# The input bias of a fused GRU and block-attention kernel, sent by DMA instead of spread by matmuls

## The chip, the cores and the metric

The kernel runs on one core of a Trainium2 chip. The metric is the device time of one execution in microseconds (us), the median of several runs; less is better. One further execution was recorded by the hardware profiler, and every row shown here comes from such a record. The engines are TensorE (PE, its weight loads PEld), VectorE (DVE), ScalarE (ACT), GpSimd (POOL) and SyncE (SP), which here only starts transfers. GpSimd starts a few transfers too, on a queue of its own.

## What is computed

Two layers, each added to its own input; all tensors are float32. The first is a GRU over 64 steps, the second an attention over blocks of 8 steps with a projection and a layer norm.

```python
# x: [32, 64, 512]; cond: [32, 512]; W_ih, W_hh: [512, 1536]
def cell(h, x):
    gi = x @ W_ih + b_ih
    gh = h @ W_hh + b_hh
    i_r, i_z, i_n = split(gi, 3); h_r, h_z, h_n = split(gh, 3)
    r, z = sigmoid(i_r + h_r), sigmoid(i_z + h_z)
    n = tanh(i_n + r * h_n)
    return (1 - z) * n + z * h
x = x + scan(cell, cond, x)           # h of each step
block = x.reshape(32, 8, 8, 512).sum(2)
keys = rmsnorm(block @ Wk.T) * rms_weight
attn = softmax(keys @ cond[1])
proj = (attn-weighted sum of block) @ Wo.T
out = x + layernorm(x + proj) * gamma + beta
```

## The kernel before

The recurrence sets the length. A step `t` works on a 128 x 128 state: partition `j*32 + b` holds 128 of the 512 units of batch row `b`. For each step TensorE runs 16 matmuls of `h_t` (the transposed state) with `w_hh` into a bank of PSUM (`step`, L608), which is `first_ps[t]` for the first four steps and `gates_ps` for the rest. Then the gates are made by ScalarE and VectorE. While they are, TensorE computes the input's share `gi` of the step five ahead (`gi_chunk`, L571): 12 matmuls of 384 columns, from `x` and `W_ih` each split into a high and a low part, into one of two banks `gi_ps`. VectorE adds the bias tile `b_in` and moves the result to `gi_tok` (`keep_gi`, L723). SyncE moves that by DMA, SBUF to SBUF, from time-major rows to the state's layout in `gi` (`move_gi`, L240). At the end of a step ScalarE writes the next step's `gi` and bias into `gates_ps` (`seed_n`, L427, and `seed_rz`, L436), and TensorE accumulates on top.

The first four steps take their `gi` another way: the bias is laid into the four banks `first_ps[0..3]`, and the products of `x` and `W_ih` are accumulated straight onto it in full float32 (L635, four rounds `k` of 16 matmuls, each round waiting for its quarter of `W_ih`).

The two biases come in as 8 rows (`bias_rows`, 4 for `b_ih`, 4 for `b_hh`), loaded by two small DMAs into zeroed memory. A first matmul with K = 8 (`own_rows` as weights, L624) puts them in the state's layout into `first_ps[0]`; ScalarE copies that to `bias_rec`, and from there ScalarE and VectorE seed the other three banks. Behind the rounds of `W_ih` four more matmuls with K = 8 (`pick` as weights, L638) spread the rows over all 128 partitions, one chunk of 384 columns each, and ScalarE copies the four results to `b_in` (L423). TensorE waits for all four copies before the first `gi_chunk` (for step 4), and VectorE before the `keep_gi` of it.

Transfers before the first step all go through SyncE's queue in this order: the biases, `x` of the first four steps, `cond`, the four quarters of `W_ih` (768 KB each), `x` of the next four (`load_ahead(1)`), the four quarters of `W_hh`. Some wait for an earlier one to land. Then come, step by step, the moves of `gi`, the loads of `x_t` ahead, and `x1`, the same input in the other layout (`load_residual`). GpSimd waits for the last quarter of `W_hh` (L363) and then starts six transfers that copy small rows to many partitions: `gamma`, `beta`, `wq_rec`, `keys_wq`, `keys_sq` and `wq` (L368 to L372).

Places that matter to the order in time:

- Step 4 is the first that is seeded from `gi`. At `s = 3` ScalarE waits, ahead of `seed_rz`, until four moves have landed, those of steps 4, 5, 6 and 7 (L434).
- `gi_tok` has two halves. The `keep_gi` of step 6 waits until the move of step 4 has landed, that of step 7 waits for the move of step 5, and so on.
- SyncE starts its transfers in program order: move of step 4, load of `x_t`, moves of 5 and 6, load of `x1`, move of 7.

## Time and profile before

| | us |
|---|---|
| median of 3 runs | 407.91 (406.82 to 408.11) |
| profiled execution, device time | 407.7 |
| its span, first to last instruction | 405.9 |
| TensorE busy | 365.0 (90%) |
| VectorE busy | 286.1 (70%) |
| ScalarE busy | 138.0 (34%) |
| GpSimd busy | 62.1 (15%) |

In this execution the gates of step 0 begin at 29.69 us, and those of steps 1 to 4 follow at 5.00 us intervals. What comes before 29.69 us is the opening; what comes after about 346 us is attention and layer norm. All times in the sections below are us from the start of the span.
### The profile page before, as it was taken

To read this page: it belongs to the slowest core of one execution; us is meant where nothing else is said; L and a number is where in the kernel's file an instruction comes from. 1 tells how busy PE (TensorE), PEld (TensorE's weight loads), DVE (VectorE), ACT (ScalarE), POOL (GpSimd) and SP (SyncE) were. 2 spreads that over 40 slices of the span, in tenths; PEclk is the share of its full clock that TensorE was granted. 3 is DMA by queue.
4 is the path that set the end of the run, shared out by engine and by line. 5 is a ranking of instruction groups with operands and counts; after the bars stand their busy time and mean duration, and the time that the engine had idled before them with its cause. 6 is when DMAs were issued, how large, how long until landed. Compare 5 with 4: busy or idle time off the path is not lost.

```text
span 405.9 us, 9319 instructions
## 1 busy us (share of the span) xinstructions
PE 365.0 (90%) x3102; PEld 212.4 (52%) x3102; DVE 286.1 (70%) x1191; ACT 138.0 (34%) x498; POOL 62.1 (15%) x74
## 2 busy tenths in 40 slices
PE   6999999999999999999999999999999999755400
PEld 2455565656565656565656565656565643422100
DVE  1605577776777767777676767676767666999997
ACT  5411223232323232323232323232323553545532
POOL 5040010101010101000010001010101010263563
PEclk9969999999999999999999999999999999996955
DMA  6936525322222222222222221313132210000233
GB/s 265 409 46 105 152 83 159 78 65 67 66 65 65 65 65 65 65 65 65 66 63 70 59 79 51 82 48 82 53 76 60 51 41 27 2 1 1 104 156 155
DMA packets 17412, 33.89 MB, mean 84 GB/s; under 512 B 2088, under 2 KB 9904, under 8 KB 17392
## 3 DMA queue, kind: packets, MB, share of 16 engines
q1 hardware_dynamic: 16912, 32.85, 27.2%
q0 software_dynamic: 480, 0.79, 1.8%
q8 instruction: 10, 0.16, 0.2%
q14 instruction: 10, 0.08, 0.1%
HBM read 17.64 MB, written 4.19 MB: 54 GB/s over the span
## 4 chain that ended last, share of the span: by engine, by line
PE 82%; DVE 14%; POOL 1%; issue 1%; ACT 0%; POOLq 0%; DVEq 0%
PE gates_ps L608 40%; PE gi_ps L571 34%; DVE cx_all L990 5%; DVE cx_all L1011 2%; PE first_ps L635 1%; DVE cx_all L1039 1%; PE fourth_ps L635 1%; PE third_ps L635 1%; PE keys_ps L635 1%; DVE w_hh L982 1%; PE fourth_ps L608 1%; PE third_ps L608 1%; PE keys_ps L608 1%; PE first_ps L608 1%; DVE w_hh L976 1%
## 5 line engine op out<-in xcount | busy, mean ns | idle before, releaser
L608 PE MATMUL gates_ps<-w_hh,h_t 128*32 128x384 f32 x1920 | 167.3, 489 | 0.7 <-DVE h_t L745 0.6
L608 PEld LDWEIGHTS gates_ps<-w_hh,h_t 128*32 128x32 f32 x1920 | 56.7, 109 | 82.9 <-issue 50.8
L571 PE MATMUL gi_ps<-w_ih_hi,xt_hi 128*128 128x384 f32 x240 | 87.7, 365 | 0.6 <-issue 0.6
L467 ACT ACTIVATE rz<-gates_ps 128x256 f32<-128x256 f32 x60 | 23.1, 385 | 173.4 <-PE gates_ps L608 173.4
L571 PE MATMUL gi_ps<-w_ih_hi,xt_lo 128*128 128x384 f32 x240 | 81.2, 338 | 0.0
L571 PE MATMUL gi_ps<-w_ih_lo,xt_hi 128*128 128x384 f32 x240 | 81.2, 338 | 0.0
L823 DVE TENSOR_TENSOR rz<-gates_ps,rz 128x128 f32<-128x128 f32 x60 | 17.5, 292 | 80.2 <-ACT rz L467 80.2
L571 PEld LDWEIGHTS gi_ps<-w_ih_hi,xt_hi 128*128 128x128 f32 x240 | 45.5, 189 | 39.0 <-issue 39.0
L353 POOL TENSOR_TENSOR xb_all<-x,beta 128x512 f32 (+1 forms) x16 | 21.2, 1327 | 187.9 <-DVE x L753 187.9
L571 PEld LDWEIGHTS gi_ps<-w_ih_lo,xt_hi 128*128 128x128 f32 x240 | 45.7, 190 | 0.0
L571 PEld LDWEIGHTS gi_ps<-w_ih_hi,xt_lo 128*128 128x128 f32 x240 | 45.6, 190 | 0.0
L723 DVE TENSOR_TENSOR gi_tok<-gi_ps,b_in 128x384 f32<-128x384 f32 x60 | 33.0, 550 | 12.6 <-PE gi_ps L571 12.6
L745 DVE STREAM_TRANSPOSE h_t<-hist 128x32 f32<-128x32 f32 x189 | 36.4, 216 | 2.4 <-issue 0.2
L739 DVE TENSOR_TENSOR hist<-zh,n 128x32 f32<-128x32 f32 (+1 forms) x192 | 34.2, 201 | 2.2
L732 DVE SCALAR_TENSOR_TENSOR n<-rz,n 128x32 f32<-128x32 f32 (+1 forms) x192 | 31.0, 189 | 0.0
L476 ACT ACTIVATE n<-n 128x32 f32<-128x32 f32 (+1 forms) x128 | 29.0, 256 | 3.3 <-DVE n L828 3.3
L427 ACT ACTIVATE gates_ps<-bhh_n 128x128 f32<-128x128 f32 x60 | 16.9, 282 | 21.5 <-DVE rz L823 21.5
L436 ACT ACTIVATE gates_ps<-gi 128x256 f32<-128x256 f32 x60 | 22.5, 375 | 1.8
L828 DVE TENSOR_TENSOR n<-rz,gi 128x32 f32<-128x32 f32 x120 | 21.6, 222 | 0.0
L395 POOL TENSOR_TENSOR cx_all<-cx_all,xb_all 128x1024 f32<-128x1024 f32 x7 | 17.5, 2501 | 16.4 <-DVE cx_all L990 15.4
L359 POOL COPY br_all<-br_cur 128x128 f32 x7 | 2.0, 291 | 99.8 <-DVE br_turned L777 99.8
L829 DVE TENSOR_TENSOR zh<-rz,hist 128x96 f32<-128x96 f32 x64 | 16.1, 251 | 0.0
(210 smaller groups left out, 338.4 us busy)
## 6 DMA issues: line engine op xcount, KB each, us to landing
gi<-gi_tok SPq DMA_DIRECT2D x60, 192.0 KB, 3.3
x<-in_x_rec_dram SPq DMA_DIRECT2D x16, 256.0 KB, 2.8
x_t<-in_x_t_dram SPq DMA_DIRECT2D x15, 256.0 KB, 3.3
out_dram<-cx_all SPq DMA_DIRECT2D x7, 512.0 KB, 2.6
xb_all<-in_w_ih_dram SPq DMA_DIRECT2D x4, 768.0 KB, 6.0
w_hh<-in_w_hh_dram SPq DMA_DIRECT2D x4, 768.0 KB, 7.0
wo_t<-in_wo_t_dram SPq DMA_DIRECT2D x1, 1024.0 KB, 5.6
wk_t<-in_wk_t_dram SPq DMA_DIRECT2D x1, 1024.0 KB, 5.6
```

What stands on the lines that cost most here:

```text
L353: pool.tensor_tensor(xb_all[:, bass.ds(quad * Q, Q), :], x1[:], over_steps(beta), ALU.add).then_inc(xb_ready, 1)
L436: act.activation(gates_ps[:, P:3 * P], gi[:, (s // Q) % 2, first + P:first + G3], ACT.Copy).then_inc(seeded, 1)
L467: act.activation(rz[:], gates_bank(t)[:, P:3 * P], ACT.Sigmoid).then_inc(rz_ready, 1)
L476: act.activation(n[:, c], n[:, c], ACT.Tanh).then_inc(n_ready, 1)
L571: mm = pe.matmul(gi_ps[tok][:, 0:G3], a[:, k, :], w[:, k, gi_cols(j)], start=(k == 0 and a is xt_hi and w is w_ih_hi), stop=(k == NJ - 1 a ...
L608: mm = pe.matmul(gates_bank(t)[j * B:(j + 1) * B, P:], h_t[:, k * B:(k + 1) * B], chunk(w_hh, k, j), start=False, stop=(k == NJ - 1), skip ...
L723: dve.tensor_tensor(gi_tok[:, tok, :], gi_ps[tok][:, 0:G3], b_in[:, gi_cols(j)], ALU.add).then_inc(gi_tok_ready, 1)
L732: dve.scalar_tensor_tensor(out=n[:, c], in0=z[:, c], scalar=1.0, in1=n[:, c], op0=ALU.subtract, op1=ALU.mult).then_inc(terms_ready, 1)
L739: dve.tensor_tensor(hist[:, s, c], zh[:, c], n[:, c], ALU.subtract).then_inc(h_ready, 1)
L745: dve.transpose(h_t[:, c], hist[:, s, c]).then_inc(ht_ready, 1)
L828: dve.tensor_tensor(n[:, c], r[:, c], i_n[:, c], ALU.add).then_inc(n_pre_ready[number], 1)
L990: ins = dve.scalar_tensor_tensor(out=cx_all[:, c * C + t, :], in0=u_of(c, t), scalar=rstd[:, c * C + t:c * C + t + 1], in1=gamma[:], op0=A ...
```

## The change

- **`b_in`**: the four `pick` matmuls, their four ScalarE copies and the `pick` tile are gone. SyncE, once the second quarter of `W_hh` has landed, starts two transfers behind the queued quarters: `b_ih` (6 KB in memory) copied to 128 partitions, and the r and z parts of `b_hh` (four pieces of 1 KB) copied to 128 partitions. GpSimd adds the second to the first, 128 x 1024 elements, and signals `b_in_ready`. This addition stands ahead of GpSimd's six transfers.
- **`keep_gi(Q, Q)`** on VectorE (for step 4) moves from before step 0 to after step 0's last transpose, together with the wait for `b_in_ready`. TensorE no longer waits for `b_in` before the first `gi_chunk`.
- **The remaining bias matmul** gets `own_rows` and `bias_rows` of 128 partitions, zero beyond the first 8. VectorE clears `bias_rows` (128 x 512), after `zeros` and before it makes the zero operand `xt_hi`; the first bias load waits for that.
- **Zero matmuls**: two of 512 columns before the bias matmul and six behind it, into `gates_ps`, which nothing reads before step 4. `split_x(1)` on ScalarE waits for the six, since it overwrites their operand.
- The copy to `bhh_n` on ScalarE moves behind the splits.

```diff
-        bias_rows = xb_all[0:2 * NJ, 48:52, :].rearrange("p t u -> p (t u)")
+        bias_rows = xb_all[:, 48:52, :].rearrange("p t u -> p (t u)")
...
-        pick = cx_all[0:2 * NJ, 2 * NJ:3 * NJ, :]
-        own_rows = cx_all[0:2 * NJ, 3 * NJ + 1, :]
+        own_rows = cx_all[:, 3 * NJ + 1, :]
+        b_hh_rz = cx_all[:, 5 * NJ:7 * NJ, :].rearrange("p (j c) u -> p j (c u)", j=NJ)
...
             load_w_hh(3)
+            sp.wait_ge(w_hh_in[1], 16)
+            sp.dma_start(b_in[:], b_ih_d.rearrange("j n -> (j n)")[None, :].broadcast_to([P, 3 * D])
+                         ).then_inc(b_in_loaded, 16)
+            sp.dma_start(b_hh_rz, b_hh_d[None, :, 0:2 * P].broadcast_to([P, NJ, 2 * P])).then_inc(b_in_loaded, 16)
             move_gi(0, -1)
...
+            pool.wait_ge(made, 6 + 1 + 2 * NJ)
+            pool.wait_ge(b_in_loaded, 32)
+            rz_cols = b_in[:].rearrange("p (j n) -> p j n", j=NJ)[:, :, P:]
+            pool.tensor_tensor(rz_cols, rz_cols, b_hh_rz, ALU.add).then_inc(b_in_ready, 1)
             pool.wait_ge(w_hh_in[NJ - 1], 16)
...
-            act.activation(bhh_n[:], bias_rec[:, 3 * P:], ACT.Copy)
...
+            act.wait_ge(pe_warmed, Q + 1)
             split_x(1)
-            for j in range(NJ):
-
-                act.wait_ge(bias_spread, j + 1)
-                act.activation(b_in[:, gi_cols(j)], bias_ps[j][:, 0:G3], ACT.Copy).then_inc(b_in_ready, 1)
+            act.activation(bhh_n[:], bias_rec[:, 3 * P:], ACT.Copy)
...
-            pe.wait_ge(pick_made, 6)
+            def keep_warm(times):
+
+                for _ in range(times):
+                    mm = pe.matmul(gates_ps[:], xt_hi[:, 0, :], xt_hi[:], start=True, stop=True)
+                return mm
+
+            keep_warm(2)
+            pe.wait_ge(pick_made, 3)
             pe.wait_ge(bias_in, 32)
             pe.matmul(first_ps[0][:], own_rows, bias_rows, start=True, stop=True).then_inc(bias_laid, 1)
+            keep_warm(6).then_inc(pe_warmed, 1)
...
-            for j in range(NJ):
-                pe.matmul(bias_ps[j][:], pick[:, j, :], bias_rows, start=True, stop=True).then_inc(bias_spread, 1)
 
             pe.wait_ge(made, 6 + 1 + 2 * NJ)
-            pe.wait_ge(b_in_ready, NJ)
             gi_chunk(Q, Q, 1)
...
+                if peeled and s == 0:
+                    dve.wait_ge(b_in_ready, 1)
+                    keep_gi(Q, Q)
                 if not (last and t + 5 >= T):
                     keep_gi(t + 5, s + 5)
...
             dve.memset(zeros, 0.0).then_inc(zeros_made, 1)
+            dve.memset(bias_rows, 0.0).then_inc(bias_made, 1)
...
             split_x(1)
-            dve.wait_ge(b_in_ready, NJ)
-            keep_gi(Q, Q)
```

On TensorE, at the start of the program, the four zero matmuls, the bias matmul and the first round of `W_ih` stand like this before:

```order
L621 MATMUL first_ps<-xt_hi 128x512
L624 MATMUL first_ps<-xb_all,cx_all 128x512
L635 MATMUL first_ps<-xb_all,cx_all 32x384 x4
L635 MATMUL keys_ps<-xb_all,cx_all 32x384 x4
L635 MATMUL third_ps<-xb_all,cx_all 32x384 x4
```

and after:

```order
L622 MATMUL first_ps<-xt_hi 128x512
L626 MATMUL gates_ps<-xt_hi 128x512 x2
L632 MATMUL first_ps<-xb_all,cx_all 128x512
L626 MATMUL gates_ps<-xt_hi 128x512 x6
L644 MATMUL first_ps<-xb_all,cx_all 32x384 x4
L644 MATMUL keys_ps<-xb_all,cx_all 32x384 x4
```

Two zero matmuls came in ahead of the bias matmul and six behind it; nothing else moved there.

On TensorE again, between the last round of `W_ih` and the first `gi_chunk`, before (`cx_all` holds `pick`, `xb_all` the bias rows):

```order
L635 MATMUL fourth_ps<-xb_all,cx_all 32x384 x4
L638 MATMUL gates_ps<-xb_all,cx_all 128x512
L638 MATMUL gi_ps<-xb_all,cx_all 128x512 x2
L638 MATMUL small_ps<-xb_all,cx_all 128x512
L571 MATMUL gi_ps<-w_ih_hi,xt_hi 128x384
L571 MATMUL gi_ps<-w_ih_lo,xt_hi 128x384
```

and after:

```order
L644 MATMUL third_ps<-xb_all,cx_all 32x384 x4
L644 MATMUL fourth_ps<-xb_all,cx_all 32x384 x4
L572 MATMUL gi_ps<-w_ih_hi,xt_hi 128x384
L572 MATMUL gi_ps<-w_ih_lo,xt_hi 128x384
L572 MATMUL gi_ps<-w_ih_hi,xt_lo 128x384
```

The four spreading matmuls are gone, and the chunk of step 4 follows the last round directly.

On GpSimd, behind the making of the constants, before:

```order
L348 MEMSET own_n 32x1
L368 DMA gamma<-in_gamma_dram 128x1x128
L368 DMA beta<-in_beta_dram 128x1x128
L368 DMA wq_rec<-in_rms_weight_dram 128x1x128
L368 DMA keys_wq<-in_cond_dram 128x1x128
L369 DMA keys_sq<-in_cond_dram 128x4x128
L372 DMA wq<-in_rms_weight_dram 128x512
```

and after:

```order
L348 MEMSET own_n 32x1
L366 TENSOR_TENSOR b_in<-b_in,cx_all 128x4x256
L372 DMA gamma<-in_gamma_dram 128x1x128
L372 DMA beta<-in_beta_dram 128x1x128
L372 DMA wq_rec<-in_rms_weight_dram 128x1x128
L372 DMA keys_wq<-in_cond_dram 128x1x128
L373 DMA keys_sq<-in_cond_dram 128x4x128
L376 DMA wq<-in_rms_weight_dram 128x512
```

The addition came in ahead of the six transfers, and they now stand behind its wait for the two new loads.

## Rows read from the trace of the kernel before

**Rows 1.** The page's part 4, the chain that ended last, by engine.

```profile
PE 82%; DVE 14%; POOL 1%; issue 1%; ACT 0%; POOLq 0%; DVEq 0%
```

**Rows 2.** Timeline, VectorE's first two, then TensorE: start, duration, operation, idle before.

```profile
0.84 0.17 DVE L877 MEMSET cx_all<- 128x128 f32 x1 [0.84 <-PEq L1048]
1.04 0.50 DVE L879 CAST xt_hi<-cx_all 128x512 fp32r<-128x512 f32 x1
...
4.37 2.07 PE L624 MATMUL first_ps<-xb_all,cx_all 8*128 8x512 f32 x2 [0.71 <-POOL cx_all L327]
...
7.22 1.51 PE L635 MATMUL first_ps<-xb_all,cx_all 128*32 128x384 f32 x8 [0.78 <-ACT cx_all L409]
...
12.33 0.89 PE L635 MATMUL first_ps<-xb_all,cx_all 128*32 128x384 f32 x8
...
14.97 0.83 PE L635 MATMUL first_ps<-xb_all,cx_all 128*32 128x384 f32 x8
...
20.25 1.12 PE L638 MATMUL gates_ps<-xb_all,cx_all 8*128 8x512 f32 x2
...
25.68 0.66 PE L571 MATMUL gi_ps<-w_ih_hi,xt_hi 128*128 128x384 f32 x1 [0.63 <-issue]
...
29.69 2.79 PE L608 MATMUL first_ps<-w_hh,h_t 128*32 128x384 f32 x32
```

**Rows 3.** Timeline around the start of step 4: TensorE, VectorE, SyncE, ScalarE.

```profile
49.69 2.79 PE L608 MATMUL gates_ps<-w_hh,h_t 128*32 128x384 f32 x32
...
45.10 0.52 DVE L723 TENSOR_TENSOR gi_tok<-gi_ps,b_in 128x384 f32<-128x384 f32 x1
...
45.65 0.55 SPq L240 DMA_DIRECT2D gi<-gi_tok  x1
...
49.04 0.39 ACT L436 ACTIVATE gates_ps<-gi 128x256 f32<-128x256 f32 x1
```

**Rows 4.** Busy time by stretch: PE, PEld, DVE, ACT, POOL, granted clock, DMA share, GB/s.

```profile
17.00:20.00 3.00, 3.00 (x44) 1.31 (x36) 0.23 (x1) 0.00 (x0) 0.00 (x0) 1.00 1.02 417
20.00:21.00 1.00, 1.00 (x6) 0.48 (x3) 0.00 (x0) 0.00 (x0) 0.00 (x0) 1.00 0.24 98
...
23.00:24.00 1.00, 1.00 (x2) 0.33 (x1) 0.00 (x0) 0.49 (x1) 1.00 (x2) 0.50 0.00 0
...
29.00:30.00 1.00, 1.00 (x7) 0.51 (x10) 0.13 (x1) 0.00 (x0) 0.00 (x0) 0.74 1.41 61
```

**Rows 5.** GpSimd's first transfer in the timeline, and its groups by form (busy, mean ns).

```profile
22.75 0.89 POOL L368 DMA_DIRECT2D gamma<-in_gamma_dram  x1 [15.15 <-DMA w_hh<-in_w_hh_dram]
...
L395 POOL TENSOR_TENSOR cx_all<-cx_all,xb_all 128x1024 f32<-128x1024 f32 x7 | 17.5, 2501 | 16.4 <-DVE cx_all L990 15.4 <-DVE cx_all L1006 0.9
```

**Rows 6.** Queues by stretch (packets, MB, share of 16 engines): 28 to 34, then 34 to 35.3.

```profile
DMA packets 63, 0.25 MB, mean 41 GB/s; under 512 B 3, under 2 KB 3, under 8 KB 63
q0 software_dynamic: 63, 0.25, 89.2%
...
q0 software_dynamic: 95, 0.26, 51.3%
q1 hardware_dynamic: 110, 0.17, 39.5%
```

**Rows 7.** One `gi` move each: its issue in the timeline, its time to landing.

```profile
30.45 0.69 SPq L240 DMA_DIRECT2D gi<-gi_tok  x1
DMA to landing us min/median/max: 7.0/7.0/7.0
...
DMA to landing us min/median/max: 3.3/3.3/3.3
```

**Rows 8.** Transfers issued from 35 to 38: KB each, time to landing.

```profile
gi<-gi_tok SPq DMA_DIRECT2D x1, 192.0 KB, 4.0
```

**Rows 9.** TensorE late in the kernel, idle before a matmul, and the clock there.

```profile
369.66 0.58 PE L695 MATMUL small_ps<-w_hh,same_b 128*128 128x16 f32 x2 [6.71 <-DVE w_hh L957]
...
367.00:368.00 1.00, 0.00 (x0) 0.00 (x0) 1.00 (x1) 0.00 (x0) 0.57 (x1) 0.72 0.00 0
```

More of the change, by code:

```diff
@@ L140, in gru_block_attention @@
         small_ps, third_ps, fourth_ps = pb("small_ps"), pb("third_ps"), pb("fourth_ps")
-        bias_ps = [gates_ps, gi_ps[0], gi_ps[1], small_ps]
         first_ps = [pb("first_ps"), keys_ps, third_ps, fourth_ps]
@@ L151, in gru_block_attention @@
         gi_moved = [sem("gi_moved0"), sem("gi_moved1")]
-        warmed, bias_spread, bias_laid, bias_kept = sem("warmed"), sem("bias_spread"), sem("bias_laid"), sem("bias_kept")
+        warmed, bias_laid, bias_kept = sem("warmed"), sem("bias_laid"), sem("bias_kept")
+        b_in_loaded = sem("b_in_loaded")
         first_seeded, pe_warmed, zeros_made = sem("first_seeded"), sem("pe_warmed"), sem("zeros_made")
@@ L317, in _ @@
         def _(pool):
-            pool.memset(bias_rows, 0.0).then_inc(bias_made, 1)
-            pool.memset(pick, 0.0).then_inc(pick_made, 1)
             pool.memset(own_rows, 0.0).then_inc(pick_made, 1)
@@ L322, in _ @@
             for half_ in range(2):
-                pool.wait_ge(pick_made, 2 + 2 * half_)
+                pool.wait_ge(pick_made, 1 + half_)
                 pool.affine_select(out=own, in_=own, compare_op=ALU.not_equal, fill=1.0, base=-NJ * half_,
                                    pattern=[[-1, NJ], [0, B]], channel_multiplier=1).then_inc(pick_made, 1)
-                pool.affine_select(out=pick, in_=pick, compare_op=ALU.not_equal, fill=1.0, base=-NJ * half_,
-                                   pattern=[[-1, NJ], [0, P]], channel_multiplier=1).then_inc(pick_made, 1)
             pool.memset(ident[:], 0.0).then_inc(made, 1)
```

## The prediction

> **What bounds the kernel now.** I read the chain of waits first [rows 1]: TensorE holds 82% of it, and in the recurrence it works through 5.00 us steps without a gap (the gates of step 0 begin at 29.69, those of step 4 at 49.69 [rows 2, 3]). The change touches nothing inside a step, so it can only move the moment from which the steps run at that pace. I therefore read TensorE's timeline from the start [rows 2]. The opening has three costs. The first round of `W_ih` takes 5.1 us (7.22 to 12.33) where the next takes 2.64 (to 14.97): the engine had worked without a break for 5.1 us before its matmuls came at double pace. The four K=8 matmuls and the wait for their copies take from 20.1 (the end of the rounds, 12.33 + 3 x 2.6) to 25.68. And behind them the first `gi_chunk` runs at half pace, 4.0 us (25.68 to 29.69) instead of about 2.1: the granted clock was 0.50 in 23 to 24, after 3 us of 8-row matmuls, and 0.74 in the stretch in which it rose again [rows 4]. Step 0's gates then end at 29.69 + 2.79 = 32.48. I call that G0; step 4's gates begin 17.2 us behind it [rows 3]. A price for the end of the kernel is read at step 4, because from there on nothing of the opening is left.
>
> **TensorE's own part.** Without the spreading the chunk follows the rounds, and at full clock: 20.1 + 2.1 = 22.2, gates to 25.0. G0 comes 7.5 us sooner, if nothing else is late.
>
> The zero matmuls move the clock's rise. VectorE now clears 128 x 512 elements ahead of the zero operand. No row shows that; the nearest are its 128x128 clear (0.17 us) and its copy of that shape (0.50) [rows 2], so 0.17 to four times that. I take 0.5, like the copy: the zero operand is ready at 2.1, and the first bias load, issued at 1.3 now, leaves 0.3 later and all loads behind it too. Six zero matmuls of 512 columns at 1.2 GHz, 0.43 each, end at 4.7, the bias matmul (2.07 [rows 2]) at 6.7, 0.3 later than now. TensorE then goes on with six zeros instead of pausing 0.78. It has worked from 2.1 nearly without a break, so by the 5.1 us before 12.33 and the 4.0 us before 29.69 it rises at 6 to 7; most of the six then take half as long and end near 7.9, inside the wait for the seeds (8.5). Rounds: 8.5 to 18.3, the chunk to 20.4. If the clock rises as late as now, the zeros cost 1.6 us and the rounds end at 20.9, G0 25.8. Either way the fourth quarter of `W_hh` has to be there: it lands now at 22.5, 0.25 before GpSimd's first transfer [rows 5], which will be 22.8. So G0 = 22.8 + 0.65 (the last quarter of the gates) + 0.1 = 23.6 in the good case, **8.9 us sooner**. The padded rows cost nothing: matmul time goes by columns here, 8 or 128 rows.
>
> **The bias by DMA, and who waits.** The two loads carry 128 x 6 KB + 128 x 4 KB = 1.31 MB. They stand behind the `W_hh` quarters on a queue that is full until 20.2 (417 GB/s) with a few late packets afterwards [rows 4]; the late ones are why the last quarter lands only at 22.5. At 417 GB/s they need 3.15 us more, landing at 22.8 + 3.15 = 25.95. GpSimd starts 0.25 later and adds 1024 elements in 2.5 us, as in its 128x1024 group [rows 5]: `b_in_ready` at **28.75**. VectorE waits for it between step 0 and step 1, with both `keep_gi` and step 1's elementwise work queued behind. Both must be through when step 1's gates are, at G0 + 5.5; two times 0.55 us for `keep_gi` leaves a deadline of G0 + 4.4. With G0 = 23.6 this is missed by 0.75, so the steps run as if G0 were 24.35, 8.1 us sooner than now. In the late-clock case (G0 25.8) the deadline is met.
>
> **What is late next.** GpSimd's six transfers stand behind the addition. They begin at 28.75 instead of 22.75, 6.0 us later, while the steps run 8.1 earlier; they slide 14 us into the steps. Their queue q0 [rows 6] is slow in one part: from 28 to 34 it moved 0.25 MB at 41 GB/s with the engines 89% taken (this is `keys_sq`, four pieces of 512 B copied to all partitions), and its last 0.26 MB went in 34 to 35.3. Meanwhile SyncE's queue moved nothing: the `gi` move issued at 30.45 needed 7.0 us to land, an undisturbed one 3.3 [rows 7]. Shifted by 6.0, q0 is done at 41.3 and blocks from about 32.6. The move of step 4 (issued 29.3), `x_t` and the move of step 5 (30.5) should just go ahead of it. The move of 6, `x1` and the move of 7 do not; these are 640 KB. ScalarE seeds step 4 only when the moves up to step 7 have landed. In the trace that is barely met today: `keep_gi` at 45.10, issue 45.65, seed 49.04, gates of step 4 at 49.69 [rows 3]. Now these 640 KB start behind q0. At the 331 GB/s of 34 to 35.3 they would be in by 43.3; the same mix (move, `x_t`, move) took until 35.65 + 4.0 = 39.65 in the trace [rows 8], 4.35 us behind q0's end, which gives 45.65. I take 45.2, near that row, since the last move is queued already. With 0.1 + 0.39 + 0.05 for the seed, **step 4's gates begin at 45.75** instead of 49.69.
>
> The sum, against the profiled execution: 407.7 - (49.69 - 45.75) = 403.8. The runs' median is 0.2 above that execution: **404.0 us**. More than half of the 8 us won on TensorE goes into a new wait in front of step 4, about 4.2 us long (from 24.35 + 17.2 = 41.55). The late-clock case gives the same time, since that wait ends by GpSimd's transfers and not by G0.
>
> **Rivals.**
> 1. SyncE's queue is served beside q0. Against it stands the 7.0 us landing; for it, that one transfer is little evidence. The Trainium skill says so ("DMA: Bandwidth & Descriptors", Queues, rings and completion order): each engine takes turns between its queue rows, packet by packet. This trace doesn't agree, by that 7.0 us. Worked from rows: an engine that alternates passes the moves among the last slow packets and is through with all three transfers some 2.5 us sooner, 401.5; with no slow part at all the 8.1 us remain whole, 399.8. Chance 0.2.
> 2. TensorE's clock falls in the new gap. Late in the kernel TensorE was idle for 6.71 us and the clock fell 4.7 us into it (0.72 in 367 to 368) [rows 9]. The gap here is 4.2, a little under. If it falls, the next 4 to 5 us run at half pace, 2 to 2.5 us: 406.2. Chance 0.12.
> 3. The move of step 5 is caught behind q0 too. Then the `keep_gi` of step 7 waits for it until 41 to 42, where step 3's work on VectorE should begin at 39.8, and everything behind is 1 to 2 us later: 405.5. Chance 0.1.
> 4. Slower than before: the loads of the bias are as slow as `keys_sq`. All four copy a small row to many partitions, and `b_hh`'s part has its form, four pieces for each of 128 partitions. At 41 GB/s its 0.52 MB take 12.8 us instead of 1.3, `b_in_ready` comes 11.5 us later, and with it the six transfers: 415.5. The break-even is 3.9 us of extra loading, 7.1 us for both or 185 GB/s. Against it: `wq` copies a 2 KB row the same way and ran in the fast stretch from 34 to 35.3 [rows 6], and `b_ih` comes in pieces of 6 KB. Chance 0.13, spread from 406.5 upward.
>
> **How the numbers follow.** The forecast has 0.45, the rivals 0.2, 0.12, 0.1 and 0.13. The time is the likeliest case's, 404.0. Its own bounds are 43.3 to 45.65 for the last landing (402.1 to 404.5) and 0.5 us for the clear and the loads. Low end 399.6, from rival 1 whole; high end 408.5, which leaves out most of rival 4. A measurement tells 0.3% (1.2 us) from no change: faster means below 406.7. That is the forecast, rivals 1 and 3 and over half of rival 2: 0.81. Within 0.3%: the rest of 2 and the near part of 4, 0.07. Slower: 0.12.
>
> **What would show it.** In the changed kernel's timeline: rounds of `W_ih` all 2.6 us long, no clock fall before step 0, gates of step 0 ending at 23.5 to 26; the addition on GpSimd starting near 26.2 and lasting 2.5; VectorE waiting for it before the first `keep_gi`; q0 at some 40 GB/s from 34 to 40; a move of `gi` with a landing of 7 us or more; and TensorE waiting some 4 us for ScalarE's seed in front of step 4. Wrong would be: loads landing after 29 (rival 4), no wait in front of step 4 (rival 1), or gates of step 4 drawn out beyond their 2.79 us (rival 2).

## The result, and the profile after

The changed kernel takes 408.8 us (median of 20 runs, 407.16 to 410.61), the kernel before 407.2 us in the same rounds (20 runs, 405.28 to 408.39). The ratio is 1.0046, with a 95% interval of 1.0032 to 1.0060: slower by half a percent, where 404.0 and faster was forecast. The profiled execution took 408.77 us with a span of 407.0, 1.1 us longer than the one of before. The page's part 4 for it, the chain that ended last, beside [rows 1]:

```profile
PE 72%; DVE 15%; DMA 9%; SPq 1%; issue 1%; POOL 1%; ACT 0%; DVEq 0%; ACTq 0%; POOLq 0%
```

TensorE's share fell by ten points and the transfers have 9%, where before they had none. The timeline of TensorE in the changed kernel, which answers to [rows 2] and to the gates in [rows 3] (start, duration, operation, idle time before and what ended it):

```profile
7.60 0.88 PE L644 MATMUL first_ps<-xb_all,cx_all 128*32 128x384 f32 x8
...
10.23 0.87 PE L644 MATMUL first_ps<-xb_all,cx_all 128*32 128x384 f32 x8
...
18.12 0.44 PE L572 MATMUL gi_ps<-w_ih_hi,xt_hi 128*128 128x384 f32 x1
...
20.41 2.14 PE L609 MATMUL first_ps<-w_hh,h_t 128*32 128x384 f32 x24
23.23 0.85 PE L609 MATMUL first_ps<-w_hh,h_t 128*32 128x384 f32 x8 [0.68 <-DMA w_hh<-in_w_hh_dram]
...
36.98 2.79 PE L609 MATMUL fourth_ps<-w_hh,h_t 128*32 128x384 f32 x32
48.30 5.35 PE L609 MATMUL gates_ps<-w_hh,h_t 128*32 128x384 f32 x32 [5.86 <-ACT gates_ps L437]
...
56.01 2.79 PE L609 MATMUL gates_ps<-w_hh,h_t 128*32 128x384 f32 x32
...
347.18 2.79 PE L609 MATMUL gates_ps<-w_hh,h_t 128*32 128x384 f32 x32 [0.21 <-DVE h_t L751]
```

Up to 23.23 everything is as it was meant: the first round of `W_ih` takes 2.63 us instead of 5.1, the chunk follows the rounds, and step 0 begins at 20.41 instead of 29.69. Step 4 begins at 48.30, after 5.86 us of idling, only 1.4 us ahead of before; its gates take 5.35 us instead of 2.79, and by step 5 the kernel is behind. In the kernel before the last step's gates began here:

```profile
345.91 2.79 PE L608 MATMUL gates_ps<-w_hh,h_t 128*32 128x384 f32 x32 [0.21 <-DVE h_t L745]
```

So each execution splits into three numbers: the start of step 4, the 59 steps from there to the last, and the rest. Before: 49.69 + 296.22 + 59.99. After: 48.30 + 298.88 + 59.82. The change won 1.39 us, lost 2.66 us inside the steps behind it, and the small remainder lies in the end.

The other engines of the changed kernel, from its timeline; compare [rows 3] and [rows 5]:

```profile
26.68 2.37 POOL L366 TENSOR_TENSOR b_in<-b_in,cx_all 128x1024 f32<-128x1024 f32 x1 [20.97 <-DMA cx_all<-in_b_hh_dram]
29.00 0.89 POOL L372 DMA_DIRECT2D gamma<-in_gamma_dram  x1
29.08 1.02 DVE L729 TENSOR_TENSOR gi_tok<-gi_ps,b_in 128x384 f32<-128x384 f32 x2 [2.29 <-POOL b_in L366]
...
39.45 0.55 SPq L240 DMA_DIRECT2D gi<-gi_tok  x1
...
47.85 0.39 ACT L437 ACTIVATE gates_ps<-gi 128x256 f32<-128x256 f32 x1 [6.61 <-DMA gi<-gi_tok]
```

The seed of step 4 waited 6.61 us for a move of `gi` to land. That move was issued at 39.45, and the trace has this for it (who waited for it, and the time from issue to landing; undisturbed it is 3.3 [rows 7]):

```profile
  ACT gates_ps L437: 6.6, 1
...
DMA to landing us min/median/max: 8.3/8.3/8.3
```

Meanwhile, from 38 to 42, GpSimd's queue had the 16 transfer engines to itself, 92% busy at 33 GB/s; SyncE's queue moved nothing although the move of index 6, `x1` and, from 39.45, the last move were waiting:

```profile
DMA packets 32, 0.13 MB, mean 33 GB/s; under 512 B 0, under 2 KB 0, under 8 KB 32
q0 software_dynamic: 32, 0.13, 92.4%
```

The times to landing of the two large copies on that queue, changed kernel (source and issuer, count, KB, us to landing):

```profile
keys_sq<-in_cond_dram POOLq DMA_DIRECT2D x1, 256.0 KB, 11.1
wq<-in_rms_weight_dram POOLq DMA_DIRECT2D x1, 256.0 KB, 12.2
```

and before:

```profile
keys_sq<-in_cond_dram POOLq DMA_DIRECT2D x1, 256.0 KB, 9.2
wq<-in_rms_weight_dram POOLq DMA_DIRECT2D x1, 256.0 KB, 9.9
```

And the clock. The changed kernel by stretch, columns as in [rows 4]:

```profile
42.00:46.00 4.00, 0.43 (x3) 0.11 (x1) 0.58 (x5) 0.00 (x0) 0.00 (x0) 1.00 1.03 246
46.00:47.00 1.00, 0.00 (x0) 0.00 (x0) 0.45 (x2) 0.00 (x0) 0.00 (x0) 0.93 1.03 237
47.00:48.00 1.00, 0.00 (x0) 0.00 (x0) 0.97 (x2) 0.15 (x1) 0.16 (x1) 0.50 1.03 367
50.00:53.00 3.00, 3.00 (x24) 0.79 (x16) 0.00 (x0) 0.00 (x0) 0.00 (x0) 0.50 0.36 74
54.00:55.00 1.00, 1.00 (x8) 1.00 (x7) 0.87 (x6) 0.64 (x4) 0.00 (x0) 1.00 0.00 0
```

TensorE had been idle since 42.4; its clock fell from 2.4 to 1.2 GHz at 46.9 (a mean of 0.93 in 46 to 47), 4.4 us into the gap, and it was back by 54. Step 4's gates ran at half speed.

One point of the description of the kernel before has to be put right, since the experiments lean on it. `gi_chunk` of index 4 to 7, and the move of each, do not hold the input's share of step 4, 5, 6, 7. Each holds one quarter of the columns for all four steps. That is why the seed of step 4 needs all four moves; the wait can't be relaxed step by step. The waits and their times are as described. In what follows the four are called the moves 4 to 7.

### The profile page after: what moved, and what is told of

It is laid out like the page before. It is cut to its first block, busy times and chain, and to the rows that moved or that the text cites. A ratio compares the mean times of both kernels' runs of the same rounds, so it can differ in the third digit from the quotient of the medians.

```text
span 407.0 us, 9316 instructions
## 1 busy us (share of the span) xinstructions
PE 361.7 (89%) x3102; PEld 211.4 (52%) x3102; DVE 287.0 (71%) x1192; ACT 136.1 (33%) x494; POOL 62.4 (15%) x71
## 3 DMA queue, kind: packets, MB, share of 16 engines
HBM read 18.95 MB, written 4.19 MB: 57 GB/s over the span
## 4 chain that ended last, share of the span: by engine, by line
PE 72%; DVE 15%; DMA 9%; SPq 1%; issue 1%; POOL 1%; ACT 0%; DVEq 0%; ACTq 0%; POOLq 0%
PE gates_ps L609 40%; PE gi_ps L572 31%; DVE cx_all L998 5%; DMA gi<-gi_tok 4%; DVE cx_all L1019 2%; DMA xb_all<-in_w_ih_dram 2%; DMA w_hh<-in_w_hh_dram 2%; DMA cx_all<-in_b_hh_dram 2%; DVE cx_all L1047 1%; DVE w_hh L990 1%; DVE w_hh L965 1%; DVE w_hh L984 1%; POOL b_in L366 1%; DVE cx_all L1014 1%; PE gi_ps L586 0%
## 5 line engine op out<-in xcount | busy, mean ns | idle before, releaser
L609 PE MATMUL gates_ps<-w_hh,h_t 128*32 128x384 f32 x1920 | 169.8, 495 | 6.5 <-ACT gates_ps L437 5.9
L609 PEld LDWEIGHTS gates_ps<-w_hh,h_t 128*32 128x32 f32 x1920 | 57.2, 110 | 90.3 <-issue 52.7
```

Source lines behind the costliest of these rows:

```text
L609: mm = pe.matmul(gates_bank(t)[j * B:(j + 1) * B, P:], h_t[:, k * B:(k + 1) * B], chunk(w_hh, k, j), start=False, stop=(k == NJ - 1), skip ...
```

## The experiments

My theory from the two profiles: the opening was won as forecast, and lost to **GpSimd's queue**, whose slow copy `keys_sq` was put off by 6 us and now stands in the way of the moves that step 4 needs; and in the idle time in front of step 4 **the clock fell**. The rivals: that any copy to 128 partitions is slow, that the late bias on VectorE is what costs, and that TensorE's opening still counts. Each time below is a median; the ratio is to the kernel before, run in the same rounds on the same chip. The kernel before had medians from 406.1 to 407.5 us in the batches, so ratios are the safer comparison between experiments of different batches.

### The source of the slow copy (row_contig, rows_contig)

`keys_sq` reads `cond[1]`, which in the layout handed over lies in four pieces of 512 B, 16 KB apart. Here it is handed over once more as a row of its own.

```diff
-            pool.dma_start(q_row.rearrange("p (j u) -> p j u", j=NJ),
-                           cond_d.rearrange("(j b) u -> b j u", j=NJ)[1:2].broadcast_to([P, NJ, P])
-                           ).then_inc(consts_in, 16)
+            pool.dma_start(q_row, q_d[None, :].broadcast_to([P, D])).then_inc(consts_in, 16)
```

> The changed kernel, except that keys_sq is loaded from a row of 512 contiguous values (cond[1], handed over as an input of its own) instead of four pieces of 512 B that lie 16 KB apart. Theory A (the new wait in front of step 4 comes from GpSimd's queue, and that queue is slow because of the form of this one transfer): q0 is done within 2 to 3 us of its last issue, by about 35; the move for step 7 lands by 43; TensorE waits under 1 us in front of step 4 and its clock stays up; step 4 begins at 42 to 43 instead of 48.3, and the time is 400 to 401, about 8 us less than the changed kernel. Rival B (any copy of a small row to 128 partitions is that slow on this queue): q0 still runs at some 40 GB/s to about 43, and the time stays at 408 to 409.

Measured: 402.38 us, ratio 0.9921 (0.9892 to 0.9949). The copy in row_contig, and what TensorE waited for up to 60 us:

```profile
keys_sq<-in_q_dram POOLq DMA_DIRECT2D x1, 256.0 KB, 7.3
...
PE gates_ps L607 <- ACT gates_ps L435: 1.7, 1, 1.7
```

Step 4 begins at 44.43, the clock stays up (granted clock 1.00 from 40 to 45), and the 59 steps from there to the last take 296.22 us again. The same 256 KB go to the same place on the same queue, so neither of these alone made the copy slow; the rival falls. But the forecast of 400 to 401 was missed by 1.4: the queue was not done by 35 but by 39.6, so part of its slowness is not the source's. rows_contig changed the source of `keys_wq` too:

```diff
-                                 (q_row_rec, cond_d.rearrange("(j b) u -> j b u", j=NJ)[:, 1, :])):
+                                 (q_row_rec, q_d.rearrange("(j u) -> j u", j=NJ))):
```

> The changed kernel with both keys_sq and keys_wq loaded from the contiguous row (row_contig changed keys_sq alone). In row_contig the 16 slow packets of keys_wq (up to 1.0 us each) are left, q0 ends at 39.6 and TensorE waits 1.67 us in front of step 4. Theory A (pieces 16 KB apart are what is slow): no packet of q0 takes over 0.6 us, q0 ends by 36.5, the wait in front of step 4 falls below 0.7 us, step 4 begins at 42 to 43.3, and the time is about 1.3 us less than row_contig's, 401. Rival (something else in that stretch slows q0): step 4 stays at 44 to 44.5 and the time at 402.4.

Measured: 403.11 us, ratio 0.9934 (0.9908 to 0.9960), step 4 at 44.23. The rival was right here: the pieces of `keys_wq` are not what is left. From 31 to 38 the copies and the moves run side by side, and both are slow, whatever the source (for the moves of that stretch see late_consts below).

### The same edit in the kernel before (before_rows_contig)

Both edits of rows_contig, in the kernel before.

> The control: the kernel before, with keys_sq and keys_wq loaded from the contiguous row and nothing else. Theory A (a slow q0 costs only where the moves for steps 5 to 7 meet it; in the kernel before only the move for step 4 does, with 10 us in hand): q0 is done by 30, the move for step 4 lands in 3 to 4 us, step 4 still begins 20.0 us behind step 0, and the time is the same within 0.3%. Rival (a slow q0 costs by itself): 1 us or more faster.

Measured: 406.99 us, ratio 1.0013 (0.9988 to 1.0038): the same. Yet the copy itself lands far sooner:

```profile
keys_sq<-in_q_dram POOLq DMA_DIRECT2D x1, 256.0 KB, 4.0
```

Here it has landed before any move does, in 4.0 us instead of 9.2; move 4 lands in 5.4 us instead of 7.0, where I had given 3 to 4. So the slow copy costs nothing measurable where no move that is soon needed meets it.

### The place of the copies (consts_first, late_consts)

consts_first puts GpSimd's addition behind its six transfers; late_consts leaves the source alone and starts four of the six behind the first `quad_work`, after step 3:

```diff
+            pool.wait_ge(consts_in, 16 * 2)
+            quad_work(0)
...
             pool.wait_ge(consts_in, 16 * 6)
-            quad_work(0)
```

Between the two stand the copies of `wq_rec`, `keys_wq`, `keys_sq` and `wq`, the last four. And for consts_first:

```diff
-            pool.wait_ge(made, 6 + 1 + 2 * NJ)
-            pool.wait_ge(b_in_loaded, 32)
-            rz_cols = b_in[:].rearrange("p (j n) -> p j n", j=NJ)[:, :, P:]
-            pool.tensor_tensor(rz_cols, rz_cols, b_hh_rz, ALU.add).then_inc(b_in_ready, 1)
...
+            pool.wait_ge(made, 6 + 1 + 2 * NJ)
+            pool.wait_ge(b_in_loaded, 32)
+            rz_cols = b_in[:].rearrange("p (j n) -> p j n", j=NJ)[:, :, P:]
+            pool.tensor_tensor(rz_cols, rz_cols, b_hh_rz, ALU.add).then_inc(b_in_ready, 1)
```

> The changed kernel, except that GpSimd starts its six transfers before it adds the two bias parts, not after. Theory A (what costs is where q0's slow stretch falls against the moves for steps 5 to 7): the slow stretch is back at 27 to 35, the bias is ready 1 us later (about 30), the move for step 4 needs 7 us again, but the move for step 7 meets no slow queue; step 4 begins at 45 to 46.5, no fall of the clock, 403 to 405. Rival (the bias arriving late on VectorE is what costs): step 4 begins 1 us later than in the changed kernel, at 49 or more, and the time is 409.5 or more.

> The changed kernel with the slow source left as it is, but GpSimd starts wq_rec, keys_wq, keys_sq and wq only after its first quad_work, that is, behind step 3; gamma and beta stay where they are. Theory A (the place in time is what matters): no q0 packet meets the moves for steps 4 to 7, step 4 begins at 42 to 43; the slow stretch of 7 us then falls into steps 4 and 5, where a move may take 7 us and more, since the next quad needs its last move only at step 7; 400 to 401.5. Rival (the slow stretch costs its time wherever it stands): the wait comes back at step 8, 404 or more.

consts_first measured 407.36 us, ratio 1.0025 (1.0005 to 1.0045), 2 us above the top of what I gave. The wait in front of step 4 is gone and a new one stands in front of step 3. What TensorE and VectorE waited for, up to 60 us:

```profile
PE fourth_ps L609 <- DVE h_t L751: 4.2, 1, 4.2
...
DVE gi_tok L729 <- DMA gi<-gi_tok: 7.0, 1, 7.0
DVE gi_tok L729 <- POOL b_in L376: 3.4, 1, 3.4
```

Move 4 is now the one caught behind the copies. VectorE waits 7.0 us for it before it may write `gi_tok` for move 6, with its elementwise work of step 2 queued behind that wait; TensorE stands 4.2 us, its clock falls, and step 3's gates take 5.02 us:

```profile
42.38 5.02 PE L609 MATMUL fourth_ps<-w_hh,h_t 128*32 128x384 f32 x32 [4.19 <-DVE h_t L751]
...
40.00:41.00 1.00, 0.00 (x0) 0.00 (x0) 0.61 (x2) 0.00 (x0) 0.00 (x0) 0.55 0.30 65
```

A mean of 0.55 in 40 to 41 puts the fall at 40.1, only 1.9 us after TensorE went idle at 38.19. Step 4 begins at 49.62. So the copies cost about as much one step earlier. The rival, the late bias on VectorE, has its sign in the start of step 4 (49 or more) but not in the time (409.5 or more): the bias came 1.1 us later here, and step 2 began 1.1 us later (33.12 instead of 31.98); the rest is the wait for move 4.

late_consts measured 402.14 us, ratio 0.9893 (0.9859 to 0.9926). TensorE's waits up to 60 us:

```profile
PE gi_ps L575 <- DVE gi_tok L732: 1.6, 1, 1.6
PE first_ps L612 <- DMA w_hh<-in_w_hh_dram: 0.9, 1, 0.9
PE gates_ps L612 <- ACT gates_ps L440: 0.8, 1, 0.8
```

The slow copy is as slow as ever (9.4 us to landing), now beneath steps 4 to 6, and neither TensorE nor the clock notices. The time is 0.6 us above the 400 to 401.5 that I gave, and step 4 begins at 45.44, not at 42 to 43; but this profile is of the slowest of its six runs (405.19), in which the bias itself was late (GpSimd's addition at 28.76 instead of 26.68). Its chain of waits up to step 4 shows what is left of the wait, 0.85 us:

```profile
33.09 7.42 DMA gi<-gi_tok
...
41.03 0.57 DVE gi_tok L732
...
41.61 3.30 DMA gi<-gi_tok
...
45.00 0.40 ACT gates_ps L440
```

Move 5 takes 7.4 us to land, VectorE waits for it before it writes `gi_tok` for move 7, and move 7 lands in 3.3 us, where in the changed kernel it took 8.3. The 5.0 us between these two are what the wait lost, 0.85 instead of 5.86. Moves 4 and 5 are as slow here (5.1 and 7.4 us) as in the changed kernel (4.8 and 7.3), although none of the four copies had been started; what slows those two is open.

Two independent edits, the source or the place, each give back most of the loss: 5.1 and 6.2 us by the ratios, 6.4 and 6.7 by the medians. That the copies started by GpSimd cause all but about 1 us of the wait is shown; `keys_sq` by its source alone is worth 4.2 us of it (5.86 to 1.67).

### The zero matmuls (no_zeros)

The changed kernel with one zero matmul instead of eight.

```diff
-            keep_warm(2)
...
-            keep_warm(6).then_inc(pe_warmed, 1)
+            keep_warm(1).then_inc(pe_warmed, 1)
```

> The changed kernel with one zero matmul (behind the bias matmul) in place of the eight; the padding to 128 rows stays. Theory A (the end of the wait in front of step 4 is set by GpSimd's transfers, so that nothing won earlier on TensorE counts): the rounds of the input weights end about 2 us later, gates of step 0 end at 24 to 25.5, step 4 begins at 48 to 48.5 as before, and the time is that of the changed kernel, 408.8 within 0.6. Rival (TensorE's opening still counts): 2 us slower, 410.8.

Measured: 408.91 us, ratio 1.0072 (1.0044 to 1.0101), against 1.0046 (1.0032 to 1.0060) for the changed kernel. The intervals overlap, and the changed kernel itself measured 1.0075 when it was run again (below). So no difference is shown; the rival's 2 us are at the edge of what the intervals allow. In the profiled execution the clock happened to rise at about 5, before any round, so this profile doesn't show the late rise; step 4 began at 48.39, after a wait of 5.88 us, again where GpSimd's queue lets it. What the seven other zero matmuls buy in the changed kernel is too little to be measured here.

### The padding alone, and without it (before_padded, before_zeros)

before_padded is the kernel before with only the padding (and the order of clearing and constants that goes with it) and the zero matmuls; `b_in` still comes from the four spreading matmuls. before_zeros has the zero matmuls, but 8-row operands.

```diff
-        pick = cx_all[0:2 * NJ, 2 * NJ:3 * NJ, :]
-        own_rows = cx_all[0:2 * NJ, 3 * NJ + 1, :]
+        pick = cx_all[:, 2 * NJ:3 * NJ, :]
+        own_rows = cx_all[:, 3 * NJ + 1, :]
...
+            keep_warm(2)
             pe.matmul(first_ps[0][:], own_rows, bias_rows, start=True, stop=True).then_inc(bias_laid, 1)
+            keep_warm(6).then_inc(pe_warmed, 1)
```

> The kernel before, with only the padding and the zero matmuls of the change: own_rows, pick and bias_rows have 128 rows, two zero matmuls stand ahead of the bias matmul and six behind it; b_in still comes from the four spreading matmuls, and GpSimd's transfers start at 22.5 to 23 as they did. Theory A: the clock stays up through the spreading, which takes about 3.5 us instead of 5.5; the first gi_chunk takes 2.1 instead of 4.0; gates of step 0 end at 26 to 27, and since q0's slow stretch (27 to 35) does not meet the move for step 7, step 4 begins at 43.5 to 45; the time is 401 to 403. Rival (the gain on TensorE is lost again to the moves wherever it is made): step 4 begins at 47 or later, 405 or more.

> The kernel before with the eight zero matmuls (two ahead of the bias matmul, six behind), but with all bias matmuls still of 8 rows: before_padded without the padding. Theory A (8-row matmuls let the clock fall, 128-row ones hold it): the clock rises early as in before_padded (by 8), falls again within the four spreading matmuls or right behind them, and the first gi_chunk runs at half pace, 3.5 to 4 us; step 0 begins at 26.5 to 28, the time is 1 to 2.5 us above before_padded's 404.6, so about 406. Rival (the zeros alone do it, the padding does nothing): as before_padded, step 0 at 24.8, 404.6.

before_padded: 404.61 us, ratio 0.9959 (0.9935 to 0.9983). before_zeros: 406.86 us, ratio 0.9992 (0.9967 to 1.0017). The spreading, the first chunk and step 0 in before_padded:

```profile
18.70 0.59 PE L650 MATMUL gates_ps<-xb_all,cx_all 128*128 128x512 f32 x1
...
22.50 0.41 PE L574 MATMUL gi_ps<-w_ih_hi,xt_hi 128*128 128x384 f32 x1 [0.63 <-issue]
...
24.76 2.79 PE L611 MATMUL first_ps<-w_hh,h_t 128*32 128x384 f32 x32
```

and in before_zeros, with the clock behind the spreading:

```profile
22.58 1.21 PE L647 MATMUL small_ps<-xb_all,cx_all 8*128 8x512 f32 x2
...
24.42 0.66 PE L572 MATMUL gi_ps<-w_ih_hi,xt_hi 128*128 128x384 f32 x1 [0.63 <-issue]
...
28.53 3.54 PE L609 MATMUL first_ps<-w_hh,h_t 128*32 128x384 f32 x32
...
24.00:25.00 1.00, 0.58 (x2) 0.61 (x3) 0.00 (x0) 0.32 (x1) 1.00 (x2) 0.50 0.19 55
```

With 128 rows the chunk takes 2.3 us, with 8 rows 4.1. It is the same data and the same columns, and in these two profiles the clock stayed at 2.4 GHz behind the padded matmuls and fell behind the others, as it did in the kernel before [rows 4]. Theory A for the padding holds in the profiles; the times agree with it (2.25 us apart), but the two intervals just overlap. The zero matmuls by themselves are worth nothing measurable. In before_padded step 0's gates end at 27.55, half a microsecond later than expected; step 4 begins at 44.97, as expected, and TensorE doesn't wait for it. Its total is 1.6 us above the 401 to 403 that I gave, of which the profile shows 1.35: its stretch behind the last step is 61.34 us instead of 59.99. The same is seen in the profiles of before_zeros (61.33), late_consts (61.36), after_again (61.4) and hold_again (61.34); in all five the clock is at 0.50 for 3.4 us, beginning 5.4 to 6.1 us behind the start of the last step. Which executions have it, I can't tell from single profiles.

### The clock in front of step 4 (hold_clock, hold_again, after_again)

The changed kernel with 27 matmuls into a free bank, in front of step 4's waits.

```diff
+                if first and s == Q:
+                    for _ in range(27):
+                        pe.matmul(keys_ps[:], xt_hi[:, 0, :], xt_hi[:], start=True, stop=True)
                 if not (isinstance(t, int) and t < Q):
                     wait(pe, seeded, t * 2 + 2 - 2 * Q)
```

> The changed kernel with 27 zero-effect matmuls (512 columns, into a bank that is free) on TensorE in front of step 4's waits; they fill 5.8 us of the 5.9 us in which it stood idle. Theory A (the idle gap let the clock fall, and that made step 4 and its chunk slow): the granted clock stays 1.00 through step 4, its gates take 2.79 instead of 5.35 us, step 5 begins 5.1 us behind step 4 instead of 7.7, and the time is 2.2 to 2.6 us less than the changed kernel's 408.8, so 406.2 to 406.6. Rival (the clock costs nothing, what counts is the seed): 408.8.

Measured: 407.64 us, ratio 1.0039 (1.0016 to 1.0062). That is 1.2 us below the changed kernel by the medians and only 0.3 by the ratios, where 2.2 to 2.6 was expected. In its profile the steps from 4 to the last took 296.25 us instead of 298.88, as expected, but step 4 began 0.83 us later. So both kernels were run again, side by side.

> The changed kernel, unchanged, on the same chip and in the same rounds as hold_again, to give hold_clock's difference without a change of chip and to show how much the end of the wait in front of step 4 varies (48.30 in the first profile). Theory A (the clock's fall costs 2.6 us in every execution): 2.2 to 2.7 us above hold_again. Rival B (the extra matmuls of hold_clock make the transfers later, and give back half): 1 to 1.5 us above it, with step 4 again 0.8 us earlier than in hold_again. Rival C (in many executions the clock does not fall at all): under 1 us above it, and step 4 at the same time in both.

> hold_clock, unchanged, beside after_again. Theory A: 2.2 to 2.7 us below after_again, step 4 at 48 to 49.2. Rival B (the 27 matmuls put the landing of the last move back): 1 to 1.5 us below, and step 4 at 49 or later, 0.8 us behind after_again's. Rival C: under 1 us below, step 4 at the same time in both profiles.

Measured together: after_again 410.05 us, ratio 1.0075 (1.0054 to 1.0095); hold_again 407.77 us, ratio 1.0010 (0.9993 to 1.0027). The difference is 2.28 us with the intervals well apart, and this time hold_again's step 4 is the earlier one (48.76 against 49.55), so rival B is not borne out. Theory A's range is met. But by the profiles the 2.28 us are not all the clock's: the steps from 4 to the last take 297.75 us in after_again and 296.60 in hold_again, 1.15 us less, and 0.79 is the start of step 4. After_again's clock fell at 45.9, 2.1 us into a gap of 5.79, and was back at 52.7, within step 4's gates (4.32 us long). What a fall costs differs from execution to execution: with the clock up step 5 begins 5.12 us behind step 4 (row_contig), and in the four profiles of the changed kernel and its near relatives with a fall in front of step 4 it begins 6.65 to 7.88 us behind, which is 1.5 to 2.8 us more. That a fallen clock makes step 4 slow and that matmuls in the gap keep it up is shown; how much that is in the median is known only as 0.3 to 2.3 us, from two comparisons that don't agree. This is hold_again's clock where the changed kernel's had fallen:

```profile
47.00:48.00 1.00, 1.00 (x6) 0.81 (x6) 0.61 (x1) 0.00 (x0) 0.00 (x0) 1.00 1.02 251
50.00:53.00 3.00, 3.00 (x29) 1.91 (x22) 0.97 (x6) 1.03 (x5) 0.00 (x0) 1.00 0.66 128
```

### What is left, and the order of the transfers (after_x1_behind, late_row_contig, late_contig_x1)

In the changed kernel `x1` (256 KB) is started ahead of move 7. after_x1_behind exchanges the two for the first quad.

```diff
-                    if s % Q == 2:
+                    if s % Q == 2 and not (first and s == 2):
...
+                    if first and s == 2:
+                        load_residual(0)
```

> The changed kernel with one edit: the load of x1 for the first quad is started behind the move of index 7 instead of ahead of it. Theory A (the wait in front of step 4 ends when the transfers queued behind GpSimd's have gone, in the order in which they were started): the last move lands 1 to 1.7 us sooner, step 4 begins at 46.6 to 47.3 instead of 48.3, the clock falls in the gap as before or just misses, and the time is 1 to 2 us below the changed kernel, 406.8 to 407.8. Rival (the last move is bound by VectorE's own wait, not by the load): 408.8.

Measured: 408.75 us, ratio 1.0052 (1.0030 to 1.0074), no change. Move 7 still took 8.2 us to land, and TensorE waited 5.75 us. Everything up to 30 us ran 1.2 us late in this profile (GpSimd's first transfer at 30.23 instead of 29.00), and from there the distance to step 4 was 19.4 us against 19.3. My picture of a queue in which 256 KB less in front means an earlier landing is not borne out. What holds the last move, beyond the end of GpSimd's copies, is open. A candidate that neither the forecast nor a run has is `wo_t`, a load of 1 MB that SyncE starts at 40.04, 0.6 us behind the last move: from 42 to 47.75 SyncE's queue moved 1.22 MB, and the moves 6 and 7, `x1` and the move of index 8 are only 0.85 of them. Against it stands that in the kernel before and in late_consts `wo_t` follows move 7 as closely, and that move landed in 3.3 us.

late_row_contig has the edits of late_consts and row_contig together; late_contig_x1 has that of after_x1_behind besides.

> late_consts and row_contig together: the changed kernel with wq_rec, keys_wq, keys_sq and wq started behind the first quad_work, and keys_sq from the contiguous row. Theory A (both edits remove the same wait): the gain doesn't add up; step 4 begins 21.0 to 21.5 us behind step 1's predecessor as in late_consts, and the time is 401.5 to 402.5, like late_consts (402.1). Rival (the slow stretch behind step 4 still costs something in late_consts): 1 us or more below it, 401 or less.

> late_row_contig with one more edit: the load of x1 for the first quad is started behind the move of index 7 instead of ahead of it. Theory A (what is left of the wait in front of step 4 is the last move queued behind that 256 KB load): the wait of 0.85 us in late_consts disappears, and the time falls by 0.5 to 0.9 against late_row_contig. Rival (the last move is late because VectorE writes it late, after waiting for an earlier move to land): no change.

late_row_contig: 402.10 us, ratio 0.9879 (0.9846 to 0.9911), 5.3 us below the kernel before in its rounds and like late_consts; the two edits remove the same wait. late_contig_x1: 403.12 us, ratio 0.9900 (0.9874 to 0.9926), no further gain; its profile has the same 0.9 us in front of step 4, as its rival says: the last move is late because VectorE writes it late, after move 5 (see the chain of late_consts). late_row_contig, late_consts and row_contig beat both kernels; their intervals overlap, so which of them is best is not settled.

## Why the prediction was wrong

**What held.** Up to step 2 the forecast's times came true. Forecast, and measured in brackets: the zero operand ready 0.5 us later (0.3) and the loads 0.3 later (0.3); the clock up at 6 to 7 (about 6); rounds ending at 18.3 (18.1); the last quarter of `W_hh` at 22.8 (23.2); `b_in_ready` at 28.75, by its own terms 28.7 (26.68 + 2.37 = 29.05); step 3's gates at 36.6 (36.98). One of these was luck: four rounds of 2.6 us from 8.5 would end at 18.9 and not at 18.3, but the rounds began at 7.60, and the two errors cancel. Nothing hangs on it, since step 0 waits for `W_hh`. The bias copies were fast, against rival 4: landed at about 26.5, 0.6 us later than summed. That a new wait would stand in front of step 4, who would end it and why, was forecast, and TensorE did wait for the seed, the seed for the moves, and the moves for q0.

**Step 1 that failed: "Shifted by 6.0, q0 is done at 41.3".** This took a stretch of the old profile and moved it unchanged. GpSimd's first transfer did shift by 6.25. But in the kernel before q0 had had the engines to itself; now move 4, the load of `x_t` and move 5 ran in the same stretch, and the copies became slower. That this overlap is what slowed them is likely and not shown: in before_padded and late_consts moves ran beside them too, and `keys_sq` took 9.8 and 9.4 us against 9.2 and 11.1. `wq`, the last copy, landed 12.2 us after its issue instead of 9.9, at 44.9 where the sum has 26.46 + 9.9 + 6.0 = 42.4. Move 7 landed at 47.75 instead of 45.2. The term "wait in front of step 4, 4.2 us" measured 5.86, and step 4 began at 48.30 instead of 45.75: 2.55 us. In late_consts, with the four copies out of the way, 0.85 us of the wait is left, and the last move lands in 3.3 us instead of 8.3; so 5.0 us of the 5.86 come from those transfers, by way of the last move.

**Step 2 that failed: rival 2, "the gap here is 4.2, a little under", chance 0.12.** The forecast took the one fall that it had in its rows, 4.7 us into an idle gap [rows 9], as a limit under which a gap of 4.2 us would stay. The row itself was misread by a little: the gap begins at 369.66 - 6.71 = 362.95 and the mean of 0.72 puts the fall at 367.44, 4.5 us into it. And it is no limit. In the profiles the clock fell 4.4 us into the gap (changed kernel), 4.7 (after_x1_behind), 3.4 (no_zeros), 2.1 (after_again) and 1.9 (consts_first), the last in a gap of 4.19 us, as long as the one that was forecast. So a rightly sized wait could have cost the fall as well, and the fall belonged into the main sum instead of beside it with 0.12. It cost 2.66 us in the profile; I had given 2 to 2.5. With both terms the sum is 403.8 + 2.55 + 2.66 = 409.0, less 0.2 for the end, 408.8, the profiled execution. That it closes is arithmetic, since the terms are read from that same execution.

**The range.** Its upper end, 408.5, was made from rival 4 and from rival 2 taken one at a time. The measured 408.8 is the forecast's own mechanism with its two late terms together. A sum with two late terms that can come together needs an upper end from both.

**The other rivals.** Rival 1, the queues served side by side, is half right: from 31 to 38 packets of both did pass in the same microseconds, from 38 to 42 only q0's did. The Trainium skill's rule ("DMA: Bandwidth & Descriptors", Queues, rings and completion order) of taking turns by packet fits the first stretch and not the second, 32 packets of q0 and none of q1 in 4 us with a move outstanding; why, no run here shows. Rival 3, move 5 late, happened in part: VectorE waited 1.39 us for it ahead of step 3's work, and step 3 did not suffer; but move 5 is as late in late_consts without the copies, so q0 is not shown to be the cause.

**The base.** The profiled execution of before (407.7) lay in the upper part of its 20 runs (405.28 to 408.39), so a gain counted from it was overstated by some 0.5 us. In before_rows_contig's profile, which took 405.18 us, step 0 begins at 27.10 where [rows 2] have 29.69, with everything behind it alike. The opening before seems to vary between these two; one profile of each doesn't show how often.

## What to carry to other kernels

When an edit moves a transfer, don't shift its time from the old profile: list what else will be in flight at the new place, and give both sides a price for meeting it. Where a forecast leaves TensorE waiting for some microseconds, price the fall of its clock in the same case instead of keeping it as a separate one; a single fall in the old profile gives no length of wait that is safe. And ask of a small copy that nobody waits for which needed transfer it will meet: here a few copies, harmless in their old place, took back with the clock's fall all of a gain of some 8 us at the opening.

## What the runs showed of the hardware that I had not expected

- A copy of one 2 KB row to 128 partitions took 4.0 us to land from a contiguous source (before_rows_contig) and 9.2 us from four pieces of 512 B that lie 16 KB apart (the kernel before); no move landed while either was under way. With moves beside it, it took 7.3 us from the one source (row_contig) and 9.4 (late_consts), 9.8 (before_padded) and 11.1 us (changed kernel) from the other.
- Moves from SBUF to SBUF that land in 3.3 us undisturbed took 8.3 and 10.6 us in the changed kernel when they were issued behind such copies (moves 7 and 6), and the copies needed 2 us more there themselves. The two moves ahead of them took 4.8 and 7.3 us, but no less without the copies (5.1 and 7.4, late_consts).
- The time that TensorE had been idle when its clock fell was not the same from execution to execution: 1.9, 2.1, 3.4, 4.4 and 4.7 us in five profiles, in gaps of 4.19, 5.79, 5.88, 5.86 and 5.75 us. In row_contig's gap of 1.67 us it didn't fall.
- Rows of zeros made a difference to the clock: behind four matmuls with 8 rows it was down at 1.2 GHz (0.50 in 24 to 25, before_zeros), behind the same four padded to 128 rows, of which 120 are zero, it was not (before_padded; 2.3 us against 4.1 us for the chunk that follows). This is one profile of each.
